# Top-64 attention in an eight-layer kernel: values lag an item, copies change places, row statistics move to the stage before

## What is computed

```python
def _L2_xattn_ref(q, k, v, mask, topk, wq_w, wq_b, ...):     # topk = 64
    qh = _split_heads(q @ wq_w.T + wq_b)                     # kh, vh alike, from the context
    scores = jnp.einsum('bhqd,bhkd->bhqk', qh, kh) / np.sqrt(DHEAD)
    ...
    vals, idx = jax.lax.top_k(scores, topk)
    scores = jnp.full_like(scores, neg).at[bI, hI, qI, idx].set(vals)
    probs = jax.nn.softmax(scores, axis=-1)
    ctx = jnp.einsum('bhqk,bhkd->bhqd', probs, vh)
    ctx = ctx.transpose(0, 2, 1, 3).reshape(q.shape[0], q.shape[1], HID)
    return ctx @ wo_w.T + wo_b
...
x = x + jnp.tanh(g_xattn[2]) * _L2_xattn_ref(_layernorm(x), ctx_1024, ctx_1024, mask, 64, ...)
```

## Time and profile before

| what | value |
|---|---|
| median of 3 runs | 897.32 us (896.64 to 900.05) |
| the profiled execution | 897.16 us, of which the trace spans 895.4 us |
| busy over the span | PE 89%, DVE 73%, ACT 56%, POOL 59% |
| stage of the top-64 attention | items 0 to 31 on DVE from 273.7 to 488.4 us |
| mean granted clock of PE | 0.968 of full speed |

### The profile page before, as it was taken

One profiled execution on the slowest core, in us unless ns is written; L12 is line 12 of the kernel. 1 busy time (PEld: TensorE's weight loads), 2 busy tenths in 40 slices (PEclk: granted clock), 3 DMA queues, 4 the chain that ended last, 5 costly groups with the idle time before them and its releaser, 6 DMA issues.

```text
span 895.4 us, 18961 instructions
## 1 busy us (share of the span) xinstructions
PE 801.0 (89%) x5858; PEld 628.7 (70%) x5858; DVE 655.2 (73%) x2739; ACT 497.2 (56%) x1287; POOL 531.4 (59%) x721
## 2 busy tenths in 40 slices
PE   6999998998788676867887989999999999998897
PEld 5677775886566444645666779788778879987775
DVE  4888686888979999999999873455455542516887
ACT  5778764568997797978877331222112122226673
POOL 3565644676752978878775125456455545237883
PEclk9999999999999697979999899999999999999999
DMA  9200001000000082000222621222222243140011
GB/s 296 62 1 2 2 1 48 1 1 1 1 1 1 2 328 97 1 25 2 71 72 87 227 72 36 37 42 43 37 42 43 36 87 58 19 107 1 13 36 48
DMA packets 37823, 46.70 MB, mean 52 GB/s; under 512 B 4327, under 2 KB 33871, under 8 KB 37724
## 3 DMA queue, kind: packets, MB, share of 16 engines
q1 hardware_dynamic: 29243, 35.77, 11.9%
q0 software_dynamic: 8480, 9.72, 7.1%
HBM read 33.80 MB, written 11.68 MB: 51 GB/s over the span
## 4 chain that ended last, share of the span: by engine, by line
PE 64%; DVE 14%; ACT 8%; issue 6%; POOL 6%; another core or an unknown queue 1%; DMA 1%; DVEq 0%; ACTq 0%; POOLq 0%; SPq 0%
PE ps L3012 10%; PE ps L3023 10%; PE ps L2358 4%; PE ps L2454 3%; PE ps L2481 3%; PE ps L2780 3%; PE ps L2800 3%; PE ps L3067 2%; PE ps L3041 2%; PE ps L2439 2%; ACT ptall L1254 2%; PE ps L2466 2%; DVE experts L1812 1%; PE ps L2811 1%; PE ps L2866 1%
## 5 line engine op out<-in xcount | busy, mean ns | idle before, releaser
L2080 DVE COPY ptall<-experts 128x512 f32 x136 | 53.3, 434 | 97.8 <-PE ps L3012 49.1
L1388 ACT ACTIVATE wk<-ps 128x1024 f32<-128x1024 f32 x34 | 34.9, 1025 | 131.3 <-PE ps L3012 69.1
L3012 PE MATMUL ps<-xnT,ptall 128*128 128x128 f32 x896 | 105.0, 275 | 2.3 <-DVE ptall L2080 1.8
L3012 PEld LDWEIGHTS ps<-xnT,ptall 128*128 128x128 f32 x896 | 102.4, 192 | 3.0 <-issue 3.0
L3023 PE MATMUL ps<-experts,wk 128*128 x448 | 102.0, 381 | 1.4 <-ACT xkeep L1398 1.4
L3023 PEld LDWEIGHTS ps<-experts,wk 128*128 128x128 f32 x448 | 82.9, 190 | 17.0 <-issue 6.8
L848 POOL DMA_INDIRECT xn<-expert_in,rown x34 | 36.0, 1058 | 80.7 <-PE ps L2998 57.1
L646 POOL TENSOR_TENSOR experts<-experts,rden 128x616 f32<-128x616 f32 x32 | 38.9, 1217 | 46.8 <-DVE rden L1572 46.8
L872 POOL DMA_INDIRECT token_sum<-xkeep,dest x28 | 47.6, 1699 | 31.1 <-ACT xkeep L1398 22.5
L1229 ACT ACTIVATE experts<-experts 128x77 f32<-128x77 f32 x248 | 62.1, 258 | 0.0
L2358 PE MATMUL ps<-ones 128*128 128x256 bf16 x434 | 55.7, 286 | 5.8 <-POOL mone L599 5.8
(11 more groups left out here) (382 smaller groups left out, 2358.5 us busy)
## 6 DMA issues: line engine op xcount, KB each, us to landing
experts<-in_ew SPq DMA_DIRECT2D x16, 1024.0 KB, 8.5
xkeep<-in_bw SPq DMA_DIRECT2D x2, 1024.0 KB, 7.3
expert_in<-xkeep SPq DMA_DIRECT2D x8, 256.0 KB, 3.9
x<-token_sum SPq DMA_DIRECT2D x8, 256.0 KB, 3.8
out<-x SPq DMA_DIRECT2D x7, 256.0 KB, 2.2
x<-in_x SPq DMA_DIRECT2D x1, 1536.0 KB, 9.1
token_sum<-x SPq DMA_DIRECT2D x4, 256.0 KB, 2.6
token_sum<-x SPq DMA_DIRECT2D x1, 1024.0 KB, 4.5
```

The lines of the kernel that those rows point to most:

```text
L2080: ins = nc.vector.tensor_copy(tilew[:, v, c, :], experts[:, bass.ds(e * EW + (c * FF + v * 512), 512)])
L3012: ins = nc.tensor.matmul(ps[j % 2][:, v, k * P:(k + 1) * P], tilew[:, v, c, k * P:(k + 1) * P], xTb[j % 3][:, c, :], start=c == 0, stop=c ...
```

## The change

It does three things, all of them moves; no computation changes.

1. **ACT:** in iterations 3 to 31 the turned probabilities that are copied are those of item k-3, right behind `top_scores(k+1)` and ahead of the exponentials; in 31 item k-2 follows at the old place, so that the last items are as before. `top_out(k-3)` goes from ahead of `top_scores(k+1)` to behind the exponentials.
2. **PE:** `top_values` lags by an item (k-3) and stands right behind `top_scores(k+2)`. `top_turn` and `top_queries` of the next pair go from the end of iterations 3, 4, 5 (modulo 8) to ahead of `top_probs` in iterations 4, 5, 6, the same iterations in which ACT copies them out. `warm(14, 4)` is left out in the four iterations 26 to 29 that make an output tile.
3. **DVE:** `top_stats(1)`, the statistics of the second pair, goes from between items 1 and 2 to iterations 16 and 17 of the middle stage, one batch in each.

```diff
@@ ACT, loop over k of the top-64 stage
-                    if k >= 3 and (k - 3) // 2 % 2:
+                    if k >= N4 and (k - 3) // 2 % 2:
                         top_out(k - 3)
...
                     if 1 <= k < N4 - 1:
                         top_scores(k + 1)
+                    if 3 <= k < N4:
+                        top_turned_probs(k - 3)
                     if 1 <= k < N4:
                         top_exp(k - 1, 0)
...
+                    if 3 <= k < N4 and (k - 3) // 2 % 2:
+                        top_out(k - 3)
                     if k in top_parts:
                         top_residual(top_parts[k] // 4, top_parts[k] % 4, k)
-                    if 2 <= k < N4 + 2:
+                    if N4 - 1 <= k < N4 + 2:
                         top_turned_probs(k - 2)
@@ DVE, middle stage, then the loop over items
+                    if k in (B + 8, B + 9):
+                        top_stats(1, [k - B - 8])
...
-                    if k == 1:
-                        top_stats(1)
@@ PE, top_probs: which copies of ps2 it waits for
-                    if N4 - 9 <= i < N4 - 1:
+                    if N4 - 9 <= i < N4 - 1 and i + 2 not in top_parts:
                         warm(14, 4)
-                    if q < PAIRS and j == 3:
+                    if q < PAIRS and j == 4:
...
-                    elif q < PAIRS and j in (4, 5):
+                    elif q < PAIRS and j in (5, 6):
@@ PE, loop over k
+                    if 3 <= k < N4:
+                        top_values(k - 3)
                     if k in top_parts:
                         top_final(top_parts[k] // 4, top_parts[k] % 4, k)
+                    if q + 1 < PAIRS:
+                        if j == 4:
+                            top_turn(q + 1)
+                        if j in (5, 6):
+                            top_queries(q + 1, j - 5)
                     if 2 <= k < N4 + 2:
                         top_probs(k - 2)
...
-                        top_values(k - 2)
+                        if k >= N4 - 1:
+                            top_values(k - 2)
...
-                    if q + 1 < PAIRS:
-                        if j == 3:
-                            top_turn(q + 1)
-                        if j in (4, 5):
-                            top_queries(q + 1, j - 4)
```

More of the change, by code:

```diff
@@ L2787, in top_probs @@
                 def top_probs(i):
-                    q, j = (i + 1) // ITEMS + 1, (i + 1) % ITEMS
+                    q, j = (i + 2) // ITEMS + 1, (i + 2) % ITEMS
                     pe.wait_ge(pt_s[4].sem, pt_s[4].past(i))
-                    if N4 - 9 <= i < N4 - 1:
+                    if N4 - 9 <= i < N4 - 1 and i + 2 not in top_parts:
                         warm(14, 4)
                     pe.wait_ge(nm_s, i + 1)
-                    if q < PAIRS and j == 3:
+                    if q < PAIRS and j == 4:
                         pe.wait_ge(xts[4].sem, xts[4].past(2 * q + 2))
-                    elif q < PAIRS and j in (4, 5):
-                        pe.wait_ge(q_s[4].sem, q_s[4].past(4 * q + 2 * (j - 3)))
+                    elif q < PAIRS and j in (5, 6):
+                        pe.wait_ge(q_s[4].sem, q_s[4].past(4 * q + 2 * (j - 4)))
                     for h in range(HG):
@@ L2806, in top_values @@
                     s2 = j // 2 % 2
+                    if i - 1 in l5_at:
+                        pe.wait_ge(xts[5].sem, xts[5].past(l5_at[i - 1] + 1))
                     pe.wait_ge(pt_s[4].sem, pt_s[4].past(i + 1))
@@ L2940, in _ @@
                             l5_flip_half(l5_at[k - 2], k)
-                        if k - 3 in l5_at:
-                            pe.wait_ge(xts[5].sem, xts[5].past(l5_at[k - 3] + 1))
                         if k == N4:
```

## The result

The changed kernel took 903.93 us (median of 20 runs, 899.46 to 909.61), the kernel before on the same chips 900.83 us (20 runs, 895.31 to 903.31). The ratio is 1.0047, 95% interval 1.003 to 1.0064: slower by about 4 us by the ratio (3.1 us between the medians), where I had forecast 2.8 us less. The profiled execution took 902.20 us. In it item 2 starts right behind item 1 as forecast; what is lost is lost in DVE's waits.

A forecast was written before the change was run, and what follows sets the result against it. The prediction took DVE to bound the stage. Its terms, -1.5 - 3.8 + 2.2 + 0.3 = -2.8 us, against the profiled 897.16 us gave 894.4, or 894.5 us as a median, with a range of 891.9 to 898.5.

The forecast's parts named there:

- What bounds the kernel: In the stretch of the change DVE is full, busy 203.1 of 207.0 us; only its waits and spared work can be gained.
- The limit of 3.3 us: How late ACT may start on an item before DVE feels it, worked out from item 12's wait.
- Statistics, -1.5: Second pair's statistics on DVE, moved to the middle stage: 1.59 us saved between items 1 and 2, about 0.1 us paid there.
- Waits that go, -3.8: DVE's four waits for scores, at items 12, 19, 20 and 31, all vanish with the lag: 3.8 us less.
- Turn and queries, +2.2: ACT waits for turn and queries PE makes in the same iteration; DVE loses 2.2 us, between 0 and 12.
- brings along: Lateness ACT already has on reaching the query iterations: taken as 0.8 us, between 0 and 4.0.
- The turn is shorter and just fits: Claim that ACT's iteration with the turn, unlike those with queries, fits within DVE's item of 6.36 us.
- The end, +0.3: Iteration 31, where ACT now has two copies of probabilities: 0.3 us more, between -1.0 and +1.0.
- C: Rival: PE's idle time in one piece brings half clock, slowing query iterations by 2.1 or 3.3 us; 904 us, chance 0.06.
- B: Rival: ACT brings 2 us or more into each pair's query iterations, DVE waits 6 us; 898.3 us, chance 0.24.
- A: Rival, the full gain: ACT swallows the query iterations without loss to DVE; 892.3 us, chance 0.2.
- The first sign of being wrong: Listed with the expected profile: the forecast is wrong if DVE's waits exceed 3.8 us again.

The follow-up runs named there:

- e3: The kernel before without the 14 idle multiplications in the four iterations 26 to 29 that make an output tile: 897.31 us, ratio 0.9983.
- e2: The changed kernel with the second pair's statistics back between items 1 and 2: 903.97 us, ratio 1.0056.
- e8: Apparently (the text does not tie the label outright) the changed kernel with ACT's copy of queries behind the second half of the exponentials: 901.15 us, ratio 1.0022.
- e10: The changed kernel with ten idle multiplications on PE ahead of the values of items 8, 9, 16 and 17: 903.65 us, ratio 1.0035.
- e14: The changed kernel with queries ahead of the output tile, ten idle multiplications ahead of four items' values, and ACT's later copy of queries: 896.28 us, ratio 0.9963.
- e4: The changed kernel with turn and queries ahead of the output tile on PE: 903.08 us, ratio 1.0032.
- e13: The changed kernel with queries ahead of the output tile and ten idle multiplications ahead of the values of items 8, 9, 16 and 17: 898.66 us, ratio 0.9982.

## Why the prediction was wrong, by its own steps

- **What bounds the kernel**: right. The stage is DVE's, and the whole difference lies in its waits. The limit of 3.3 us, read from one item, gave the waits of items 15 and 16 to within 0.1 us.
- **Statistics, -1.5**: the cover held and item 2 gained its 1.6 us, but alone they showed no gain (1.0005); in the trace item 31 and the end took it back. I had written "if items 2 and later don't wait instead", and then booked the term in full.
- **Waits that go, -3.8**: right in the changed kernel's trace. The waits of items 12, 20 and 31 are gone, that of item 19 fell from 0.92 to 0.19 us, and without queries only 0.8 us was left of all. But not all of it is the lag's: item 31's wait went as well with the idle multiplications of four iterations alone (e3), and item 20 waited 0.9 to 1.1 us again in e2, e8, e10 and e14.
- **Turn and queries, +2.2**: here it failed, by size. The waits of 1.5 and 2.8 us were 1.66 and 3.00, and iterations of 7.4 and 9.0 us took 7.63 and 9.23: right. What ACT "brings along" I put at 0.8 us between bounds of 0 and 4.0; it was 2.66. With 0.8 the third pair loses 1.1, with 2.66 it lost 3.3. Two steps went into that, and a late start: ACT was 1.1 us late before the turn's iteration, which added 1.6. "The turn is shorter and just fits": at full clock it does (6.2 us and 0.9 late in e10), but the turn's iteration ran at half clock and took 7.95. And a dependency I hadn't followed: `top_abs(i)` writes the buffer from which PE turns the probabilities of item i-2. In the old order ACT had copied these out before it came to `top_abs(i)`, so that the wait was long over; with the lag it copies them behind `top_abs(i)`, and PE has only just made them, behind whatever else the iteration holds. ACT waited 4.4 us for it, 0.81 and 1.22 of it in the two turns' iterations and the rest later. The term measured 7.1 us for the two pairs, 8.1 with item 8. By e10's third pair some 1.7 us a pair, 3.4 in all, are the order at full clock, and the other 3.7 the half clock's. This is an estimate from single traces: e2's third pair, at full clock too, waited only 1.0.
- **The end, +0.3**: in the changed kernel's trace right (16.6 against 16.4), in the other traces with the lag 1 to 3 us too low.
- **Rivals**: C, slower by the clock, had named half of the cause, PE's idle time in one piece and half clock, but put it on the queries, 2.1 and 3.3 us more for each. In the changed kernel's trace these ran at full clock, and the half clock lay on the turns' iterations and the start of the next. Slow queries came in e4, e10 and e13 (2.97, 2.61 and 3.66 us instead of 1.99); in e4 the wait for them rose from 1.66 to 4.64. Its price of 904 us looks like the time measured, but partly by chance: the kernel before ran at 900.83 us in this comparison, not at the 897.32 I started from, so C said 6.8 us more and it was 3 to 4; and it put 9.6 us on the clock, which took some 3.7. Its chance of 0.06 rested on "turn and queries themselves fill the idle time", but the idle stretch lies ahead of them, and with that stretch filled they got full clock (e10, e13, e14). B (898.3) had the right direction and stopped at 2 us brought along. A was out of reach of this change; e14 came 3.3 us under the kernel before, of the 5 us that A had.
- **The range** ended at 898.5, 1.2 us above the time before; 903.9 is outside, and so are the 3.1 us between the two medians. It had left out C, although the bound "3 x 4 = 12" of the term itself reached past it. The ratio of 1.0047 lies just inside the 0.5% that I had called no change, with an interval on both sides of that line. The first sign of being wrong came: DVE's waits passed 3.8 us again.

## What to carry to other kernels

When an engine's work is moved behind a step of another engine in the same iteration, add up that engine's iterations one after the other from the first long one, not the special iteration alone: lateness below the limit costs nothing and is still there when the next long iteration comes. Follow every buffer that the moved step reads to its next writer; a lag turns an old, long satisfied dependency into a live one. And where a change gathers PE's idle time into one piece, price the work right behind it at half clock as the likely case: here it was so in eight of ten turns' iterations.

## What the runs showed of the hardware

The half clock moved when one idle stretch was filled: with ten idle multiplications the third pair's turn had 1.00 instead of 0.50, and in the fourth pair the fall came two iterations behind the turn instead (0.72 over 431 to 437 us, and again in 426 to 432 us of e13). The Trainium skill ("TensorE: Matmul & The Clock Gate", section "Part 1: The HAM clock gate") holds that half clock is the resting state and activity lifts it; the 1.00 against 0.50 agrees. A fall is therefore no fixed price of a place: the same copy of queries waited 1.66 or 4.64 us in two pairs of one execution, and the same third turn had full clock in two traces and half clock in three. It also hid two useful edits: e4 and e10 each looked nearly worthless by the total, and together with the late copy they were worth 7.5 us. Idle multiplications work on both sides: 14 of them took 1.69 us at full clock and 3.17 at half, in the chain, and without them DVE's addition behind the last items waited 4.35 us instead of 2.08.
